# Four graph layers on one core: the PNA pass turns back first and stores by pairs of aggregates, the mask row is stored last, and padding chunks are not gathered

## The reference, cut to what matters

```python
m = jnp.concatenate([h[dst], h[src]], axis=-1) @ W_pre + b_pre
mean = jax.ops.segment_sum(m, dst, num_segments=n) / deg
mean_sq = jax.ops.segment_sum(m * m, dst, num_segments=n) / deg
mn = jnp.where(has, jax.ops.segment_min(m, dst, num_segments=n), 0.0)
mx = jnp.where(has, jax.ops.segment_max(m, dst, num_segments=n), 0.0)
aggr = jnp.concatenate([mean, mn, mx, std], axis=-1)
```

## Time and profile before

| | |
|---|---|
| median of 3 runs | 4795.61 us (4791.09 to 4798.91) |
| the profiled execution's own time | 4793.74 us |
| its span, from first to last instruction | 4791.8 us |
| busy share of the span: PE, DVE, ACT, POOL | 67%, 67%, 49%, 70% |
| mean granted clock of TensorE, as a share of full speed | 0.704 |
| indirect DMAs on POOL: GAT, sum, PNA, GATv2 pass | 832, 762, 782, 832 |

### The profile page before, as it was taken

The page is one execution under the profiler, slowest core; times in us unless marked ns, Lnnn a source line. Parts: engine busy times, 40 slices in busy tenths (PEclk is TensorE's granted clock), DMA queues, the critical chain, the costliest instruction groups (busy, mean ns, idle before and its releaser), DMA issues. The chain is left out here.

```text
span 4791.8 us, 79159 instructions
## 1 busy us (share of the span) xinstructions
PE 3212.9 (67%) x19497; PEld 2744.2 (57%) x19497; DVE 3210.8 (67%) x7496; ACT 2330.2 (49%) x4887; POOL 3374.4 (70%) x3434
## 2 busy tenths in 40 slices
PE   4888888887433343345555555665497888888886
PEld 3666666666433333334455555555465777777776
DVE  5888888887533333345678777777666676666666
ACT  4766666664200000003566666666535566666665
POOL 4777777774767777776777777777522777777774
PEclk7555555556655655567777777777798788888887
DMA  7333333331212222221677777777742333333333
GB/s 140 87 88 88 87 88 88 87 87 33 68 47 55 55 56 56 56 54 56 198 255 251 253 250 247 259 248 253 244 119 51 90 83 80 82 81 81 81 82 74
DMA packets 368491, 567.61 MB, mean 118 GB/s; under 512 B 107124, under 2 KB 171287, under 8 KB 368052
## 3 DMA queue, kind: packets, MB, share of 16 engines
q1 hardware_dynamic: 254190, 332.06, 21.9%
q0 software_dynamic: 106912, 228.04, 19.6%
q10 hardware_dynamic: 6950, 2.44, 0.2%
HBM read 329.39 MB, written 230.89 MB: 117 GB/s over the span
## 5 line engine op out<-in xcount | busy, mean ns | idle before, releaser
L2113 POOL DMA_INDIRECT m_G<-dr_tab,chunk_src x782 | 884.0, 1130 | 247.2 <-issue 238.1
L893 POOL DMA_INDIRECT e_G<-dr_tab,src_idx x832 | 796.4, 957 | 273.2 <-issue 238.3
L893 POOL DMA_INDIRECT v_G<-dr_tab,src_idx x832 | 791.6, 951 | 253.9 <-issue 245.9
L1891 POOL DMA_INDIRECT s_G<-dr_tab,chunk_src x762 | 719.2, 944 | 253.3 <-issue 243.8
L1999 PE MATMUL s_OUT<-s_G,s_S 128*128 x1664 | 373.9, 415 | 582.1 <-POOLq L1884 539.5
L1999 PEld LDWEIGHTS s_OUT<-s_G,s_S 128*128 128x128 f32 x1664 | 348.5, 319 | 607.2 <-issue 607.2
L2255 PE MATMUL m_BK<-eye,m_XT 128*128 128x128 f32 x3136 | 529.6, 335 | 248.0 <-ACT m_XB L2171 237.7
L1945 DVE TENSOR_TENSOR ACC<-ACC,s_OUT 128x129 f32 x832 | 241.1, 290 | 612.3 <-PE s_OUT L1999 500.6
L2255 PEld LDWEIGHTS m_BK<-eye,m_XT 128*128 128x128 f32 x3136 | 469.8, 177 | 290.7 <-ACT m_XB L2171 260.7
L2171 ACT COPY m_XB<-m_BK 128x512 f32<-128x512 f32 x784 | 421.9, 603 | 418.2 <-PE m_BK L2255 415.3
L1321 PE MATMUL e_OUT<-e_RH,e_S 128*128 128x144 f32 x1664 | 511.6, 476 | 2.1 <-DVE e_RH L1207 2.1
(11 more groups left out here) (377 smaller groups left out, 7086.5 us busy)
## 6 DMA issues: line engine op xcount, KB each, us to landing
dr_ends<-m_XB SPq DMA_DIRECT2D x392, 512.0 KB, 4.8
e_LR<-dr_row_loc SPq DMA_DIRECT2D x104, 256.0 KB
v_LR<-dr_row_loc SPq DMA_DIRECT2D x104, 256.0 KB
m_SAME<-dr_row_same SPq DMA_DIRECT2D x98, 256.0 KB
s_G<-dr_tab ACTq DMA_DIRECT2D x1408, 0.5 KB
s_G<-dr_tab SPq DMA_DIRECT2D x1408, 0.5 KB
e_G<-dr_tab,src_idx POOLq DMA_INDIRECT x832
v_G<-dr_tab,src_idx POOLq DMA_INDIRECT x832
```

Of the source, the lines that this page charges most:

```text
L893: pool.indirect_dma_start(out=out, out_offset=None, in_=table, in_offset=bass.IndirectOffsetOnAxis(ap=g["src_idx"][:, step:step + 1], axis ...
L1891: pool.indirect_dma_start(out=G[:, c % (RING * GROUP), 0:D], out_offset=None, in_=table[:, :], in_offset=bass.IndirectOffsetOnAxis(ap=g["c ...
L2113: pool.indirect_dma_start(out=G[:, k % Q, c % GROUP, :], out_offset=None, in_=table[:, :], in_offset=bass.IndirectOffsetOnAxis(ap=g["chunk ...
```

## The change

Five edits, in the order of the diff.

1. **No padding.** `gather_step` issues nothing for steps 830 and 831, and `chunks_of` nothing for chunks 782 and 783. The waits count what really lands (`landings`). So each of the GAT, sum and GATv2 passes has two fetches less, all at its end. (The PNA pass had none of these before.)
2. **Mask row last.** In the sum pass SP loads the row numbers and fetches rows by register first, and waits for the mask and stores it behind its eleventh chunk.
3. **Mask loads of the PNA pass.** SP loads the mask of group k+3 in front of the stores of group k, once the scans of group k-1 are done (before: group k+4, once those of group k are done).
4. **Stores by pairs of aggregates.** The four stores of a group now hold four chunks and two aggregates each: first sums with minima, first and second half, then maxima with squares, first and second half. The first two wait for the copies of the minima only. A contiguous piece is 1 KB instead of 2 KB; the bytes are the same. ScalarE's wait for the free half of `m_XB` moves with it: it now waits in `back(k, 0)` and in `back(k, 2)` for the store of the same half of group k-2.
5. **Turns back first.** TensorE does `turn_back(k, 0..3)` and then `turn(k + 2)`.

```diff
+REAL_STEPS = CHUNKS + TILES - 1
...
 def gather_step(g, pool, table, out, step, gathered):
 
+    if step >= REAL_STEPS:
+        return
     pool.indirect_dma_start(out=out, out_offset=None, in_=table,
...
+def landings(k):
+
+    return 16 * (min((k + 1) * GROUP, REAL_STEPS) - k * GROUP + k // 4 * GROUP)
...
-                    dve.wait_ge(gathered[b], base[b] + 16 * GROUP * (i + 1))
+                    dve.wait_ge(gathered[b], base[b] + landings(k))
...
-                        pe.wait_ge(gathered[b], base[b] + 16 * GROUP * (i + 1))
+                        pe.wait_ge(gathered[b], base[b] + landings(k))
...
-            return [c for c in range(j * GROUP, (j + 1) * GROUP) if c not in SP_CHUNKS and c not in ACT_CHUNKS]
+            return [c for c in range(j * GROUP, min((j + 1) * GROUP, CHUNKS)) if c not in SP_CHUNKS and c not in ACT_CHUNKS]
...
+                rows_by_register(sp, mybir.EngineType.SP, 0)
                 sp.wait_ge(same_done, 2)
                 sp.dma_start(g["row_same"].rearrange("(k p e) -> p k e", p=P, e=P), SAME[:]).then_inc(same_out, 16)
-                rows_by_register(sp, mybir.EngineType.SP, 0)
                 sp.wait_ge(same_out, 16)
...
                 for k in range(PICKS):
-                    if k + 4 < PICKS:
-                        sp.wait_ge(scanned, PARTS * (k + 1))
-                        same(k + 4)
+                    if 1 <= k and k + 3 < PICKS:
+                        sp.wait_ge(scanned, PARTS * k)
+                        same(k + 3)
                     for q in range(PAIRS):
-                        sp.wait_ge(xb_done, halves(k, PARTS - 1) + q // 2 + 1)
-                        sp.dma_start(rows[:, k * GROUP + 2 * q + 1:k * GROUP + 2 * q + 3, :],
-                                     XB[:, k % 2, 2 * q:2 * q + 2].rearrange("p s m d -> p s (m d)")).then_inc(stored[k % 2][q], 16)
+                        m, h = q // 2 * 2, q % 2
+                        sp.wait_ge(xb_done, halves(k, m + 1) + h + 1)
+                        sp.dma_start(rows[:, k * GROUP + 4 * h + 1:k * GROUP + 4 * h + 5, m * D:(m + 2) * D],
+                                     XB[:, k % 2, 4 * h:4 * h + 4, m:m + 2].rearrange("p s m d -> p s (m d)")).then_inc(stored[k % 2][q], 16)
...
-                        if m == 0 and k >= 2:
-                            for q in (2 * h, 2 * h + 1):
-                                act.wait_ge(stored[k % 2][q], 16 * (k // 2))
+                        if m % 2 == 0 and k >= 2:
+                            act.wait_ge(stored[k % 2][m + h], 16 * (k // 2))
...
                 for k in range(PICKS):
-                    for m in range(PARTS - 1):
+                    for m in range(PARTS):
                         turn_back(k, m)
                     if k + 2 < PICKS:
                         turn(k + 2)
-                    turn_back(k, PARTS - 1)
```

More of the change, by code:

```diff
@@ L1365, in gat_pass @@
         for b in range(4):
-            g["rows_gathered"][b] += 16 * GROUP * (GROUPS // 4)
+            g["rows_gathered"][b] += landings(GROUPS - 4 + b)
 def gatv2_pass(nc, g, table, minus_xr, ACC, att):
```

## The result

The changed kernel's median is **4768.64 us** (4763.87 to 4772.54, 5 runs) beside 4793.29 us for the kernel before: a ratio of 0.9945, 95% interval 0.9931 to 0.996, which is 0.55% faster. The forecast was 4767 us. The profiled execution took 4766.75 us, with a span of 4764.7 us (before: 4791.8).

What follows compares the result with a forecast made beforehand. POOL was taken as the bound, issuing fetches back to back every 1.24 us in all four passes. 17.2 + 7.1 + 4.5 = 28.8 us off 4793.7 gives 4764.9, plus 1.9 for the median: 4767 us, range 4751 to 4781.

Steps and rivals of the forecast that it cites:

- The mask row, -17.2: Sum pass: fetching SP's rows before storing the mask shrinks POOL's 17.5 us gap to 0.30 us, saving 17.2 us.
- No padding, -7.1: Ends of GAT, sum and GATv2 passes: two fetches less each, saving 2.2, 2.5 and 2.4 us.
- Mid-pass 0 (±10): PNA mid-pass: scans start earlier, but the mean stall over all fetch offsets stays 1.51 us: 0, 10 us either way.
- falls badly: Rival, PNA mid-pass: fourth scan locks to fetches, raising the stall; 4813 us at a mean of 1.95 us; chance 0.07.
- falls well: Rival, PNA mid-pass: the fourth scan's mean stall drops to 1.3 us, giving 4749 us; chance 0.07.
- The PNA pass's end, -4.5: PNA end: earlier scans and first stores start the last store run sooner, saving 4.5 us, bounds 2.2 and 7.
- The gap neither stayed nor moved: Rival, sum pass: POOL's gap stays or turns up at another chunk by register, giving 4784 us; chance 0.08.
- The stores as the cause of the long fetches: Rival, PNA pass: stores hold the fetches, and two bursts per group double the 145 us, giving 4912 us; chance 0.01.
- the Trainium skill's inference on descriptors: PNA fetches: a VectorE instruction with two SBUF inputs doesn't hold descriptor writing, so the 145 us would have another cause.

Runs made afterwards that it cites:

- kernel 3: The kernel before with the fourth turn back ahead of the next turn and nothing else: 4789.48 us, ratio 0.9988.
- kernel 4: The kernel before with only the stores by pairs, their mask loads and ScalarE's waits: 4796.81 us, ratio 1.0001.
- kernel 1: The kernel before with the mask row stored last and nothing else: 4778.01 us, ratio 0.9966.
- kernels 5 and 6: Changed kernel with squares in PSUM, scanned first: 4615.37 us; changed kernel with the running-sums scan also reading both inputs from SBUF: 4922.9 us.
- 1 to 3: Three single-edit kernels against the kernel before: mask row last (ratio 0.9966), no padding (4785.61 us, 0.9979), turns back first (0.9988).
- 4 and 6 to 9: Stores by pairs alone (4796.81 us); two SBUF scans (4922.9); both PNA edits on the kernel before (4780.98); changed kernel with mask first (4772.63); changed kernel again (4761.92).
- kernel 10: The changed kernel with the mask row stored first again, rerun beside the changed kernel: 4775.38 us, ratio 0.9974 to the kernel before.

## Why the prediction was right, step by step

**The mask row, -17.2: right.** Place, cause and size hold. Timed alone it is -16 (-22 to -11), in the sum pass's stretch -15 to -17.6. No later chunk by register opened a gap in its place: behind the pass's first fetch no wait of POOL ahead of a fetch is over 1 us.

**No padding, -7.1: right, somewhat small.** From the table, kernels with padding against those without (all kernels, means): the GAT fetches with what follows them 1161.9 against 1159.7, -2.2 as forecast. VectorE now takes the GAT pass's last group without a wait, which is where the earlier trace rows put the limit:

```profile
1126.81 0.35 DVE L1164 TENSOR_REDUCE e_Z<-e_DP 128x64 f32<-128x192 f32 x1
```

In the sum pass -2.7 with the mask's gap and -1.7 without it (-2.5). The GATv2 pass with its end is 4.1 us shorter against a forecast of 2.4, but its fetches come out near 1041.7, 1044.5 or 1048 us, whatever the kernel, so that 1.7 us of this pass are less than its scatter. Alone the edit gave -10 us (-14 to -6).

**Mid-pass 0 (±10): right, for the stated reason.** The offsets changed, and the mean over them did not: a stalled fetch loses 1.52 us before and 1.50 after (96 stalls in both traces). The rivals "falls badly" and "falls well" need 1.77 and 1.3 for each of the 98 groups, where 1.49 and 1.47 were measured. The scans do start earlier, by 3.1 us behind the last fetch's start (10.4 to 7.3 us, 85 groups), where 1.9 was forecast. The other 1.2 us is the sooner landing, which no step had. POOL, with four buffers, felt none of it.

**The PNA pass's end, -4.5: right mechanism, the size too small and wrongly divided.** It measured -6.4 in the profiled pair, and -5.7 between the means of three kernels with the old pass (31.2, 31.0, 27.8) and five with both edits (23.6 to 25.1); the bounds were 2.2 and 7. The prediction let the last unbroken run of stores start 4.6 us earlier, 2.2 by the turn order and 2.4 by the earlier first stores. Windows of 0.5 us show where it starts, before:

```profile
3438.50:3439.00 0.50, 0.50 (x6) 0.40 (x5) 0.50 (x1) 0.50 (x2) 0.00 (x0) 1.00 0.00 0
3439.00:3439.50 0.50, 0.50 (x6) 0.50 (x6) 0.50 (x1) 0.50 (x2) 0.00 (x0) 1.00 0.92 348
```

and in the changed kernel:

```profile
3412.00:3412.50 0.50, 0.50 (x6) 0.38 (x5) 0.50 (x1) 0.50 (x3) 0.00 (x0) 1.00 0.00 0
3412.50:3413.00 0.50, 0.50 (x7) 0.49 (x6) 0.50 (x1) 0.50 (x3) 0.00 (x0) 1.00 0.92 315
```

Counted from the last turn, the run starts after 12.2, 12.6 and 11.0 us in the three kernels with the old pass, after 9.4 with the turns back alone, 8.0 with the stores alone, and 6.5 to 6.6 in all five with both edits. So the turn order brings 2.6 us, near its forecast, and both edits 5.4.

Two things were missing in the prediction. The last fetch's rows land sooner: the last turn stands 5.4, 4.8 and 3.6 us behind the last fetch's end in the old pass, 2.6 in kernel 3, 4.6 in kernel 4 and 2.4 to 4.1 with both edits, 1.5 us less in the mean. And the run itself takes longer with 1 KB pieces, as the rates below show, by 1.2 us. Together 5.4 + 1.5 - 1.2 = 5.7.

That is also why the stores by pairs show so little: behind the turns back they start the run 2.8 us earlier, but the wait ahead of `ENDS` is shorter by only 0.9 (25.2 against 24.3, the mean of the five). Of the rest 1.2 goes to the slower run and 0.6 to kernel 3's rows, which landed sooner still (2.6 against 3.2). In the times nothing can be told. That the untouched pass itself shows 27.8 to 31.2 means that no single pair of profiles could have sized this term to better than 3 us.

That the DMA engines are full to the end was also right, but their rate was not that of the earlier trace rows. The kernel before, in the steady part of its last run of stores:

```profile
3441.00:3449.00 8.00, 0.89 (x8) 0.64 (x6) 0.00 (x0) 3.13 (x6) 0.00 (x0) 0.72 1.03 376
```

and the changed kernel in its own:

```profile
3414.00:3424.00 10.00, 3.44 (x27) 2.61 (x25) 3.70 (x2) 5.63 (x11) 0.00 (x0) 0.93 1.03 339
```

With the engines full, 2 KB pieces move 376 GB/s and 1 KB pieces 339. By these rates the last 4.19 MB (2 x 2.10) take 12.4 us instead of 11.1, an estimate: the edit gives back about 1.2 us of what its earlier start brings. The prediction had taken 348 GB/s, an average with the run's end in it, for both. The estimate from the Trainium skill's cost of one DMA ("DMA: Bandwidth & Descriptors", Anatomy of one DMA — SWDGE (gpsimd) path) came to nearly 7. The section gives it for DMAs of GpSimd's own path, and these stores are SP's. The forecast by the full queue's rate was 4.5; the five kernels lie between, at 5.7.

**The sum.** 28.8 us was forecast and 24.7 to 26.3 measured (medians, and 0.0055 x 4790), 25.4 the second time. The parts measured alone, 16 + 10 + 4 = 30 us, are no further from it than their intervals reach. That 4767 us lies within 2 us of the measured 4768.64 is part luck. The prediction stood on the profiled execution and put the median 1.9 us above it, from three runs; with five the median before is 4793.29, below that execution. This took back 2.3 us of the 4 us by which the gain was put too high.

**The rivals.** The gap neither stayed nor moved (kernel 1). The stores as the cause of the long fetches, which the Trainium skill's inference on descriptors would have left as a candidate ("SBUF — State Buffer", Who interferes with whom), are out by kernels 5 and 6: stores of the same bytes without such a scan give no long fetch, and a second such scan doubles their number (96 to 193). So the runs go against the inference, taken as a rule for these fetches. No run separates whether a held fetch waits to read its row numbers or to write its descriptors.

## What to carry to other kernels

When one engine issues fetches back to back, look for the longest single wait in its list first, and follow a wait that the view calls "issue" to the other engine's DMA queue: one store in SP's list, standing in front of loads with a deadline, was worth more than the other edits together. Then compare the mean duration of one and the same instruction between passes: 1.13 against 0.944 us was 145 us, more than five times the whole change, and went away when the squares moved from SBUF to PSUM. Last, run a rearrangement with several parts once with each part alone: here the stores by pairs took the most code and gave nothing that can be measured.

## What the runs showed of the hardware

- An indirect fetch that POOL starts while VectorE scans (128x1024) with both inputs in SBUF ends 0.75 us behind the end of that scan. In the changed kernel 96 fetches, started 0.07 to 1.27 us into the fourth scan, are held so; two that started within its first 0.03 us are not. With the squares in PSUM and only the mask in SBUF, no fetch is held (946 ns in the mean, 1131 before). A second such scan in a group costs a little more than the first, 164 us against 145.
- The scan itself takes the same time from PSUM and from SBUF: a median of 2.32 to 2.35 us for each of the four in all three kernels. What the SBUF input costs stands only in POOL's rows.
- With the DMA engines full, stores in 1 KB pieces move 339 GB/s and in 2 KB pieces 376 GB/s. Over the 8 us that begin 2 us into the same run, other kernels show 377 to 379 (1 to 3, 2 KB) and 338 to 340 (4 and 6 to 9, 1 KB); kernel 10 shows 331 with the engines' share at 0.99.
- Either of the two PNA edits makes the fetches land 1.3 to 1.7 us sooner (5.6 to 4.3 and 4.0 us from the last fetch's start to the turn). Before, the stores of a group go out just ahead of its last fetch, and either edit moves some of them away. The fewer stand there, by and large, the sooner the rows land: in the count of experiment 4, 329, 168, 133 and 59 stores go with 5.6, 4.3, 4.4 and 4.0 us. That this is the reason is argued only: no run here took the stores away altogether, or held them back from the last fetches and changed nothing else.
